# A state-space scan with key projections beside it: TensorE issued in blocks of two states, sums one block later, key copies two states behind the decay

## What is computed

```python
def step(h, inp):
    xt, dt, bt, ct = inp
    h = jnp.exp(dt[:, :, None] * A) * h + (dt * xt)[:, :, None] * bt[:, None, :]
    y = jnp.einsum('ben,bn->be', h, ct)
    return (h, y)
...
y = jnp.swapaxes(ys, 0, 1) + W_D * x
y = y * jax.nn.silu(skip)
out = jnp.einsum('ble,de->bld', y, out_w)
```

## Time and profile before

| | us |
|---|---|
| median of 3 runs | 2716.72 |
| lowest and highest run | 2712.20, 2720.28 |
| profiled execution | 2719.7 |
| span of its profile | 2717.9 |
| scan stage in the trace | 88.7 to 531.6 |

### The profile page before, as it was taken

How to read it: one execution, slowest core, us unless ns; L and a number is a source line. 1 busy time by engine, 2 the same in 40 slices (tenths; PEclk the granted TensorE clock), 3 DMA queues, 4 the chain that set the end, 5 groups by cost and what they waited for, 6 DMA issues and landing times. The chain is left out here.

```text
span 2717.9 us, 31765 instructions
## 1 busy us (share of the span) xinstructions
PE 2431.8 (89%) x11965; PEld 1240.1 (46%) x11965; DVE 1367.0 (50%) x1957; ACT 909.5 (33%) x1868; POOL 623.5 (23%) x523
## 2 busy tenths in 40 slices
PE   7889999889999999897599799976997769999997
PEld 4344444335555555545345455443665423333332
DVE  5589989621778887732336511277445421111114
ACT  3555665303533334501112110077333312221221
POOL 0476777500000000001201100000000024444442
PEclk9899999999999999998799899988999879999998
DMA  3632222336535544424530010021000071660534
GB/s 107 197 110 90 75 83 78 102 102 232 180 121 178 176 144 112 149 101 142 186 132 0 0 43 3 0 95 81 13 1 4 9 296 51 246 274 26 220 119 156
DMA packets 96587, 301.31 MB, mean 111 GB/s; under 512 B 27018, under 2 KB 57446, under 8 KB 81724
## 3 DMA queue, kind: packets, MB, share of 16 engines
q1 hardware_dynamic: 62784, 171.06, 19.1%
q0 software_dynamic: 33664, 128.35, 13.0%
HBM read 446.13 MB, written 47.22 MB: 182 GB/s over the span
## 5 line engine op out<-in xcount | busy, mean ns | idle before, releaser
L755 POOL TENSOR_TENSOR x_rows<-ms_state,mb_C_everywhere 128x800 f32<-128x800 f32 x128 | 240.8, 1883 | 191.1 <-DVE ms_state L723 153.3
L778 PE MATMUL psum<-mb_context,mb_key_w 128*128 128x361 f32 x768 | 267.3, 488 | 17.6 <-ACT x_rows L635 11.4
L1009 PE MATMUL psum<-at_Wv,at_context 128*128 128x512 f32 (+1 forms) x576 | 265.0, 599 | 0.0
L723 DVE TENSOR_TENSOR_SCAN ms_state<-ms_decay,psum 128x800 f32<-128x800 f32 x128 | 233.0, 1820 | 34.3 <-ACT ms_decay L673 28.8
L3025 PE MATMUL psum<-tf_W,tf_x_T 128*64 128x512 f32 x1024 | 227.5, 597 | 0.8 <-DVE tf_x_T L3088 0.8
L3079 ACT ACTIVATE tf_hidden<-psum,tf_b 128x64 f32<-128x64 f32 x512 | 108.6, 362 | 355.9 <-PE psum L3036 355.9
L3047 PE MATMUL psum<-tf_W,tf_hidden 128*64 128x512 f32 x1024 | 226.4, 594 | 0.2
L778 PEld LDWEIGHTS psum<-mb_context,mb_key_w 128*128 128x128 f32 x768 | 140.8, 193 | 148.4 <-issue 43.2
L1110 ACT ACTIVATE at_prob<-psum,at_neg_max 100x722 f32<-100x722 f32 x128 | 110.5, 864 | 144.9 <-DVE at_neg_max L1172 144.7
L2960 POOL DMA_INDIRECT tf_W<-in_L_W,tt_weight_row x120 | 119.4, 995 | 161.4 <-PE psum L3025 115.8
L1172 DVE TENSOR_REDUCE at_neg_max<-psum 100x1 f32<-100x722 f32 x128 | 115.5, 903 | 79.5 <-PE psum L1030 79.3
(11 more groups left out here) (483 smaller groups left out, 3734.9 us busy)
## 6 DMA issues: line engine op xcount, KB each, us to landing
at_piece<-in_L_W_f POOLq DMA_DIRECT2D x24, 1024.0 KB, 6.2
keys_dram<-x_rows SPq DMA_DIRECT2D x128, 180.5 KB, 1.9
at_k_cols<-keys_dram SPq DMA_DIRECT2D x64, 361.0 KB, 3.2
sf_W<-in_L_W SPq DMA_DIRECT2D x16, 1024.0 KB, 7.3
tf_W<-in_L_W SPq DMA_DIRECT2D x8, 2048.0 KB, 20.0
mb_context<-in_ctxT SPq DMA_DIRECT2D x16, 541.5 KB, 4.5
at_context<-in_ctxT SPq DMA_DIRECT2D x8, 1083.0 KB, 5.3
ternary_dram<-at_piece_made POOLq DMA_DIRECT2D x14, 512.0 KB, 4.0
```

The costliest lines, as they stand in the source:

```text
L723: nc.vector.tensor_tensor_scan(state[:, n % RH, :], decay[:, g % RA, :, :].rearrange("p b l -> p (b l)"), drive, 0.0, ALU.mult, ALU.add).t ...
L755: nc.gpsimd.tensor_tensor(seen[:, n % RV, :], state[:, n % RH, :], cC[:, n, :], ALU.mult).then_inc(weighed, 1)
L778: last = nc.tensor.matmul(side("key", u, t == KE - 1)[:, 0:SH], lhsT=wk[:, k, e * P:(e + 1) * P], rhs=keys[:, h, k, :], start=(k == 0), st ...
L1009: last = nc.tensor.matmul(bank[0:rows_of(t), :], lhsT=ctxT[:, b % 2, k, t * P:t * P + rows_of(t)], rhs=wv[:, k, h * BANK:(h + 1) * BANK], ...
```

## The change

PE's program goes by blocks of two states, m = 0 to 7 in each tile: keys 2m and 2m + 1, then a delta half (blocks 0 and 1), a gate half (blocks 2 and 3) or the sum of x (block 5), then the sums of states 2m - 2 and 2m - 1, the pair of the block before. The last two sums of a tile are thus made in block 0 of the next tile, and those of the last tile behind all blocks. The numbers and the kinds of matmuls stay the same. `side_order` follows: keys 0 and 1, delta 0, keys 2 and 3, delta 1, keys 4 and 5, gate 0, keys 6 and 7, gate 1, then the other keys. In ACT's program LAG goes from 4 to 2, so that key n - 2 is copied behind the decay of state n, and key 9 (before: 7) ahead of the Silu; gate halves are taken behind keys 5 and 7, delta halves behind keys 1 and 3. DVE's and POOL's programs are the same.

```diff
--- before.py
+++ after.py
@@ -568,9 +568,11 @@
         tile_of = lambda t, i, j: t[:, bass.ds(i * 2 + j, 1), :].rearrange("p a t -> p (a t)")
         per, TURNS = 2 * N_ST, KE // 2
 
-        FINISH, SCALE, SUM_X, OPEN = 1, 6, 12, 11
-        GATE_AT, LAG = [3, 6], 4
-        DELTA_AT, CURVE_AT, ADD_AT = [1, 2], [7, 8, 10], 11
+        FINISH, SCALE, SUM_X, OPEN = 1, 6, 5, 11
+        GATE_AT, DELTA_AT, LAG = [2, 3], [0, 1], 2
+        CURVE_AT, ADD_AT = [7, 8, 10], 11
+        BLOCKS = N_ST // 2
+        ends_block = lambda n: n % 2 == 1
         JOIN = [3, 5, 7, 9]
         input_made = lambda t: t * (1 + N_ST) + 1
         joins = lambda t, n: t * len(JOIN) + JOIN.index(n)
@@ -584,10 +586,10 @@
             order = []
             for n in range(N_ST):
                 order.append(("key", n))
-                if n in GATE_AT:
-                    order.append(("gate", GATE_AT.index(n)))
-                if n in DELTA_AT and not last:
-                    order.append(("delta", DELTA_AT.index(n)))
+                if ends_block(n) and n // 2 in DELTA_AT and not last:
+                    order.append(("delta", DELTA_AT.index(n // 2)))
+                if ends_block(n) and n // 2 in GATE_AT:
+                    order.append(("gate", GATE_AT.index(n // 2)))
             return order
 
         SIDE = len(side_order(False))
@@ -679,10 +681,11 @@
                         take_key(t, n - LAG, last)
                     elif n < LAG and not first:
                         take_key(t - 1, n - LAG + N_ST)
-                    if n - LAG in GATE_AT:
-                        take_gate(t, GATE_AT.index(n - LAG), last)
-                    if n - LAG in DELTA_AT and not last:
-                        take_delta(t, j, DELTA_AT.index(n - LAG))
+                    taken = n - LAG
+                    if taken >= 0 and ends_block(taken) and taken // 2 in DELTA_AT and not last:
+                        take_delta(t, j, DELTA_AT.index(taken // 2))
+                    if taken >= 0 and ends_block(taken) and taken // 2 in GATE_AT:
+                        take_gate(t, GATE_AT.index(taken // 2), last)
                     if n in CURVE_AT and not last:
                         curve(t, j, CURVE_AT.index(n))
 
@@ -804,31 +807,38 @@
                                             start=start, stop=stop)
                 return last
 
-            def turn(i):
-                for g in range(per):
-                    j, n = g // N_ST, g % N_ST
-                    t = i * 2 + j
+            def add_state(t, n):
+                if n == 0:
+                    pe.wait_ge(finished, t + 1)
+                if n + 1 in JOIN:
+                    return
+                if n in JOIN:
+                    pe.wait_ge(joined, joins(t, n) + 1)
+                else:
+                    pe.wait_ge(weighed, t * N_ST + n + 1 + RH)
+                add(lambda p, cols: seen[p, n % RV, cols], n == 0, n == N_ST - 1).then_inc(summed, 1)
+
+            def block_of(t, m):
+                for n in range(2 * m, 2 * m + 2):
                     make_key(t, n)
-                    if n == 0:
-                        pe.wait_ge(finished, t + 1)
-                    if n + 1 not in JOIN:
-                        if n in JOIN:
-                            pe.wait_ge(joined, joins(t, n) + 1)
-                        else:
-                            pe.wait_ge(weighed, i * per + g + 1 + RH)
-                        add(lambda p, cols: seen[p, n % RV, cols], n == 0, n == N_ST - 1).then_inc(summed, 1)
-                    if n in GATE_AT:
-                        make_gate(t, GATE_AT.index(n))
-                    if n in DELTA_AT and t + 1 < KE:
-                        make_delta(t, DELTA_AT.index(n))
-                    if n == SUM_X:
-                        pe.wait_ge(x_scaled, t + 1)
-                        add(lambda p, cols: xc[p, t, cols], False, False)
+                if m in DELTA_AT and t + 1 < KE:
+                    make_delta(t, DELTA_AT.index(m))
+                if m in GATE_AT:
+                    make_gate(t, GATE_AT.index(m))
+                if m == SUM_X:
+                    pe.wait_ge(x_scaled, t + 1)
+                    add(lambda p, cols: xc[p, t, cols], False, False)
+                for g in range(t * N_ST + 2 * m - 2, t * N_ST + 2 * m):
+                    if g >= 0:
+                        add_state(g // N_ST, g % N_ST)
 
             pe.sem_inc(side_taken, RS)
             pe.wait_ge(wk_loaded, 16)
-            for i in range(TURNS):
-                turn(i)
+            for t in range(KE):
+                for m in range(BLOCKS):
+                    block_of(t, m)
+            for n in range(N_ST - 2, N_ST):
+                add_state(KE - 1, n)
```

## The result

| | before | changed |
|---|---|---|
| median of 6 runs each, us | 2718.50 | 2689.53 |
| lowest and highest | 2712.20, 2723.72 | 2686.91, 2692.78 |
| ratio (95% interval) | | 0.9895 (0.9879 to 0.9911) |
| span of the profile | 2717.9 | 2688.6 |
| scan stage, first dx to end of the last `finish` | 442.9 | 408.2 |

The scan stage itself became 34.7 us shorter. In the changed kernel lines 726, 708, 723 and 717 are the scan, `finish`, the product with B and dx; 781 is a key, 794 and 791 are gates 0 and 1, 806 a sum, 637 a key's copy, 675 the decay, 758 and 761 POOL's product and join.

A forecast was written before the change was run, and what follows sets the result against it. DVE and PE need nearly the same time, 49.6 and 49.4 us, and each waits for the other once a 53.28 us tile. Savings of 20.3 + 4.6 + 6.5 + 2.7 = 34.1 us gave 2682.6 us, own range 2675 to 2690.

The forecast's parts named there:

- The bound: Scan stage: DVE sets the tile, with one large wait, 3.65 us in tile 4, for ACT's decay of state 11.
- Switches: PE's sums in 8 groups a tile, not 12: 1.7 us less PE time, by itself no gain.
- Tiles 1 to 6: DVE's wait for ACT shrinks from 3.65 to about 0.6 us in each tile: 20.3 us saved.
- Tile 7 and the end: Tile 7 loses its wait for ACT, 4.6 us; one pair of sums after POOL's last product saves 2.7.
- Tile 0: Keys taken two states sooner bring rows of B and C sooner: 6.5 us saved, bounds nothing and 10.
- Rival 2: Tile 0 hangs on the transfers, so nothing is saved there: 2689.1 us; chance 0.15.
- The sum: Savings in the scan stage: 20.3 + 4.6 + 6.5 + 2.7 = 34.1 us.
- Signs: Among others: DVE's wait for ACT under 6 us in the stage, its wait at the end not over 3.
- Rival 1: The clock falls at PE's 1.6 us wait before sum 3 in seven tiles: 22.2 saved, 2694.5 us; chance 0.18.
- Rival 3: LAG 2 with key 8 as late as before: scan 11 waits 8.3 us in each tile, 2747 us; chance 0.05.
- Rival 5: Unseen waits, POOL behind sums or takes waiting for key stores, eat half the gain: about 2700 us; chance 0.12.
- Rival 4: Switches cost nothing, their gaps only move; key 8 comes 0.3 later in six tiles: 2684.4 us; chance 0.05.

The follow-up runs named there:

- e8: Changed kernel with gate 0 made behind the sums of block 2 and not before them: 2727.1 us.
- e4: Changed kernel with LAG 3 in place of 2: 2693.7 us.
- e9: e1 with ACT's order changed, the Silu ahead of decay 10 and the Ln behind decay 11: 2688.5 us.
- e1: Changed kernel with the pairing of sums undone in blocks 6, 7 and 0 and for x, 12 groups of sums a tile: 2685.0 us, again 2687.0.
- the repeat: The changed kernel measured once more, unaltered: 2692.4 us.
- e7: Changed kernel with LAG 3, delta 0 behind sums 14 and 15, and the sums split as in e1: 2696.9 us.
- e3: Kernel before with LAG 2 in place of 4 and nothing else: 2749.5 us.
- e2: Changed kernel with each block summing its own two states, not those of the block before: 2761.3 us.
- e10: Changed kernel, its pairs of sums kept, with ACT's order as in e9: 2692.0 us.
- e5: Changed kernel with the old LAG of 4 and the Silu moved to state 12: 2731.5 us.

## Why the prediction was right, and where it was off

**The bound, and what held it.** The reading was right: DVE sets the tile, and its one large wait hung on ACT's table loads, which hung on PE's keys. Sum 3 was forecast at 16.8 us after scan 0 and came at 16.77 (309.68 - 292.91), the copy of key 8 at 27.1 and came at 27.24, scan 11 at 34.6 and came at 34.77. e8 shows that a later PE passes to scan 11 one for one, and e4 (tiles 2 to 6) and e9 that the wait goes when the tables no longer stand behind key 8: it is the cause and not only beside it.

**Switches.** "By itself this is no gain": e1 bears it out, 50.37 us against 50.36. PE's busy time in tile 4 fell from 49.74 to 48.11 us, 1.6 where 1.7 was forecast.

**Tiles 1 to 6:** 20.3 us forecast. Their lengths fell from 320.0 to 301.0 us, so 19.1 were saved. The waits that stayed are 0.73 us, where 0.6 was assumed, which makes 0.8 of the 1.2 us; another 0.35 is the dx of tile 1, which met POOL's product.

**Tile 7 and the end:** 4.6 and 2.7 forecast, 6.2 measured from its dx to the last `finish` (59.52 to 53.36). The 4.6 came true: DVE waits for nobody in tile 7. The term that was mis-sized is the end, which gave 1.6: `finish` starts 5.92 us after scan 15 did, where 4.8 was forecast and 7.52 was before. "Only one pair of sums, at most 1.0 us, follows" POOL's last product misses two things. POOL starts product 14 after 1.63 us of waiting for sum 12, which now stands behind keys 14 and 15, and product 15 follows at once, so that it ends 0.5 later after scan 15 than before (4.27 against 3.80). And PE, after waits of 1.43 and 0.94 us, makes the last sum in 1.54 us and not 0.90, at a granted clock of 0.76 from 491 to 495. (In the repeat this sum took 1.16 us, and the last wait was 3.73 and not 4.10.)

```profile
488.64 1.82 DVE L726 TENSOR_TENSOR_SCAN ms_state<-ms_decay,psum 128x800 f32<-128x800 f32 x1
...
489.20 3.71 POOL L758 TENSOR_TENSOR x_rows<-ms_state,mb_C_everywhere 128x800 f32<-128x800 f32 x2 [1.63 <-PE psum L806]
491.13 0.90 PE L806 MATMUL psum<-x_rows,ident 64*64 64x400 f32 x8 [1.43 <-POOL x_rows L758]
492.96 1.54 PE L806 MATMUL psum<-x_rows,ident 64*64 64x400 f32 x8 [0.94 <-POOL x_rows L758]
...
494.56 2.23 DVE L708 TENSOR_TENSOR mb_conv_cols<-psum,x_rows 64x400 f32<-64x400 f32 x4 [4.10 <-PE psum L806]
```

**Tile 0:** 6.5 forecast, 9.4 measured. The step that failed is the rate of the first keys, "keys 0, 1 and delta 0 at that rate". Keys 0 and 1 together took 6.2 us (88.64 to 94.88), not 7.9, and the clock was up when they ended: delta 0 took 0.84 as later on, and keys 2 and 3 together 3.75 (95.59 to 99.34).

```profile
88.64 6.40 PE L781 MATMUL psum<-mb_context,mb_key_w 128*128 128x361 f32 x12 [6.21 <-PEq L835]
94.88 0.84 PE L800 MATMUL psum<-mb_proj,mb_wd 96*128 96x400 f32 x2
```

In the kernel before, PE stopped behind key 0 for sum 0, and both that sum and key 1 ran slowly (1.61 and 3.91 us):

```profile
95.08 1.61 PE L803 MATMUL psum<-x_rows,ident 64*64 64x400 f32 x8 [2.34 <-POOL x_rows L755]
96.62 3.91 PE L778 MATMUL psum<-mb_context,mb_key_w 128*128 128x361 f32 x6
```

The lead stays: key 3 ends at 99.34 (forecast: 103.2), key 8 is copied at 118.62 (122.4), and scan 11 of tile 0 starts at 126.16 (129.9), after a wait of 2.17 us for ACT. Of the rows of B and C only 1.3 us of waits are left. Rival 2, transfers as the bound of tile 0, is refuted by this tile's length and by DMA, which went from 0.82 to 0.90 busy and from 250 to 299 GB/s. The time of the whole kernel could not have told: rival 2's 2689.1 is nearer to the measured 2689.5 than the forecast is.

**The sum** for the stage, 34.1 against 34.7 measured, agrees in part by luck: tile 0 gave 2.9 us more than forecast, tiles 1 to 6 gave 1.2 less and the end 1.1 less. The measured 29.0 is less than both, and the difference stands behind the stage (2186.3 to 2191.8 in the profiles). I counted that part as unchanged. Its code is the same, and it varies by 3 to 4 us between executions of one program, but that scatter doesn't account for the gap. The medians fell by 29.0 us, and beside the repeat by 28.0 (2720.5 to 2692.4), 6 to 8 less than the stage did; for e1 it is 3 less both times. e7, whose profile has only 2185.5 behind the stage, is no example against it: its profiled execution (2687.5) is the fastest of four, and its median, 2696.9, lies 7 us above the 2720.4 of before less the 30.8 by which its stage is shorter. e3, with the old order, loses 3 as well. So the forecast left out some microseconds. Whether later stages got slower, or the stage was longer than usual in the one trace of the kernel before, these runs can't say, and the cause stays open.

**Signs.** Two of those named in the prediction did not come: DVE's wait for ACT in the stage is 6.9 us and not under 6, by the 2.17 of tile 0, and its wait at the end is 4.1 and not under 3.

**Rival 1,** the clock, did not come about: PE waits 1.61 us for the join in tile 4 at a granted clock of 1.00. The rule that I set beside it, from the Trainium skill (TensorE: Matmul & The Clock Gate, "A second HAM failure mode: psum-queue depth-cycling"), that short gaps between groups of matmuls make the clock go to and fro, does not describe these tiles, which have about four short gaps each. In e8 and e2, with gaps of over 3 us, the clock did fall (0.97 over e8's tile, 0.83 from 280 to 290 us in e2), and it did so at the end of tile 7 here. **Rival 3,** the lag that bites, was priced at 2747 and measured at 2749.5 in e3, but it needs the old order to come true, and its single wait of 8.3 us in each tile did not appear there; that the two numbers are so close is luck. **Rival 5,** unseen waits worth half the gain, did not appear in DVE's time in the stage. The waits that it names did grow, POOL's for sums from 17.2 to 31.3 us and ACT's for key stores from 4.7 to 12.5, but DVE waits for POOL nowhere. **Rival 4,** switches without a cost, would have been 1.8 us and can't be told from the forecast by the time; PE's busy time speaks against it, 48.11 us in tile 4 and 49.29 in e1, which has the four groups back.

## What to carry to other kernels

Before two engines that each look busy are made faster, follow one item of work across all of them by its distances from a fixed event: here nothing got cheaper that mattered, and only the point at which TensorE waits moved. Order and lag on a shared ring of buffers are one decision: how late a consumer takes a buffer bounds how far its producer can run ahead, and either changed alone was a loss. And a saving of 4 us in one stage has to be read from that stage's rows when the rest of the kernel varies by as much.

## What was not expected of the hardware

**dx takes longer while POOL's product runs.** dx is the one DVE instruction here whose row names no PSUM tile among its inputs. In the 14 profiles, in tiles 1 to 7, it takes 0.97 us where it overlaps a product of POOL by 0.05 us or less. Where it overlaps one by more, it takes longer by that overlap less some 0.1 us: 0.46 us of overlap make 1.32 (changed kernel, tile 1), 0.70 make 1.56 (e10), 1.09 make 1.94 (e5), 1.39 make 2.25 (e7). The scans and the products with B, which read PSUM too, overlap POOL all the time and keep to 1.82 and 1.00 us. The profile shows no wait for this; it has to be seen in the duration. No run tests the reason.

**A wait of TensorE can cost more than its length.** In e8 a wait of 3.9 to 4.3 us made the gate half behind it some 1.8 us longer (4.65 against 2.86) in each of tiles 1 to 7; in e2 3.1 to 3.5 us did the same to a sum and two keys (1.5 for 0.90, 4.9 for 3.91). Waits of 1.23 to 1.61 us for the join, one in each of tiles 1 to 7 of the changed kernel, did not, but 1.43 and 0.94 in close succession at its end did (1.54 for 0.90; 1.16 in the repeat), and did not in e5 and e8 (0.90). The length alone does not decide between these: 1.96 us in tile 7 of the kernel before was followed by a slow gate half, and 2.14 us in tile 2 of e3 by a sum and a key at full speed. At the start of the stage the unbroken keys came to the high clock within 6.2 us, while in the kernel before, with a wait of 2.34 us behind the first key, the next key still ran at the low one, until 100.46.
